# Embedding, state-space layer and routed feed-forward on one core: a rewritten beginning, nine weight copies on ScalarE, the last tile added by TensorE

## The reference

```
h   = W.T[x] + b + positions                    # gather from 50257 x 128
u   = layernorm(h)
Bu  = u @ B_bar.T ; xs = scan(Lambda_bar * x + Bu)   # diagonal complex, 64 states
h   = h + gelu(2 * real(xs @ C.T) + D * u)
xn  = layernorm(h)
top-2 of 8 experts by xn @ router_w.T + router_b, weights = softmax of the two
y_e = (silu(xn @ fc1a_e.T + b1a) * (xn @ fc1b_e.T + b1b)) @ fc2_e.T + b2_e
out = h + sum over the two chosen experts of weight * y_e
```

## Time and profile before

| | us |
|---|---|
| median of 3 runs | 186.21 (184.81 to 190.72) |
| profiled execution: first to last instruction (its span) | 157.3 |
| PE busy in it | 122.2 |
| DVE busy | 114.8 |
| POOL busy | 93.0 |
| ACT busy | 73.4 |
| matmul clock, mean share of full | 0.879 |

### The profile page before, as it was taken

How to read it: one execution, slowest core, us unless ns; L and a number is a source line. 1 busy time by engine, 2 the same in 40 slices (tenths; PEclk the granted TensorE clock), 3 DMA queues, 4 the chain that set the end, 5 groups by cost and what they waited for, 6 DMA issues and landing times.

```text
span 157.3 us, 3532 instructions
## 1 busy us (share of the span) xinstructions
PE 122.2 (78%) x807; PEld 96.5 (61%) x807; DVE 114.8 (73%) x480; ACT 73.4 (47%) x236; POOL 93.0 (59%) x114
## 2 busy tenths in 40 slices
PE   0067896938989968876996899999999999999300
PEld 0022355516837736743894689999999999983000
DVE  0899965899598999878647767587777778734573
ACT  3040882028167106038444356777877777760000
POOL 4778779300077677527756777777777776674000
PEclk9999699997559998589599999999999999997555
DMA  4411111991027271125315412444333111110896
GB/s 118 112 50 36 50 50 46 201 276 52 0 44 230 67 231 60 52 68 108 80 38 133 104 53 69 129 114 116 102 84 94 40 37 50 48 36 0 269 331 201
DMA packets 15093, 15.65 MB, mean 99 GB/s; under 512 B 2995, under 2 KB 11701, under 8 KB 15074
## 3 DMA queue, kind: packets, MB, share of 16 engines
q1 hardware_dynamic: 11058, 9.43, 23.6%
q0 software_dynamic: 2784, 5.28, 10.6%
q10 hardware_dynamic: 1232, 0.72, 1.5%
HBM read 9.62 MB, written 6.27 MB: 101 GB/s over the span
## 4 chain that ended last, share of the span: by engine, by line
PE 23%; issue 9%; DVE 6%; POOL 6%; DMA 5%; DVEq 1%; SPq 1%; ACT 1%; POOLq 0%; ACTq 0%
PE bank L1195 7%; PE bank L1181 7%; PE bank L1171 6%; POOL results L367 6%; DMA yres<-results 3%; DVE act_h L727 1%; PE bank L1161 1%; DMA results<-ysb,dest 1%; SPq L280 1%; DVEq L713 1%; DVE res L820 1%; PE bank L1051 1%; DVE res L824 1%; ACT rows L872 0%; DVE arg L609 0%
## 5 line engine op out<-in xcount | busy, mean ns | idle before, releaser
L356 POOL DMA_INDIRECT sorted_rows<-rows,slot x32 | 32.2, 1007 | 29.1 <-DVE slot L629 20.0
L716 DVE COPY w1b<-w_sb 128x516 f32 x39 | 18.9, 486 | 13.5 <-DVE act_h L727 5.7
L727 DVE SCALAR_TENSOR_TENSOR act_h<-bank,w1b,sil 128x128 f32<-128x128 f32 x78 | 23.6, 343 | 4.8 <-PE bank L1181 1.6
L367 POOL DMA_INDIRECT results<-ysb,dest x22 | 21.6, 983 | 7.9 <-issue 7.3
L1195 PE MATMUL bank<-w_sb,act_h 128*128 x156 | 25.1, 285 | 1.0 <-issue 0.5
L1181 PE MATMUL bank<-xT,w1b 128*128 128x128 f32 x156 | 24.6, 281 | 1.5 <-DVE act_h L727 1.4
L928 ACT ACTIVATE sil<-bank,w1b 128x128 f32<-128x128 f32 x78 | 24.4, 364 | 0.3 <-PE bank L1171 0.2
L1171 PE MATMUL bank<-xT,w1b 128*128 128x128 f32 x156 | 24.4, 280 | 0.0
L1181 PEld LDWEIGHTS bank<-xT,w1b 128*128 128x128 f32 x156 | 21.0, 195 | 2.1 <-DVE act_h L727 2.1
L1195 PEld LDWEIGHTS bank<-w_sb,act_h 128*128 128x128 f32 x156 | 20.9, 195 | 2.0 <-issue 1.9
L367 POOL DMA_INDIRECT results<-ysb,xt x17 | 16.8, 990 | 7.2 <-issue 3.7
(11 more groups left out here) (236 smaller groups left out, 189.7 us busy)
## 6 DMA issues: line engine op xcount, KB each, us to landing
w_sb<-w_all SPq DMA_DIRECT2D x8, 386.0 KB, 5.8
xt<-sorted_rows SPq DMA_DIRECT2D x39, 65.0 KB, 2.0
yres<-results SPq DMA_DIRECT2D x8, 256.0 KB, 4.9
sorted_rows<-pad SPq DMA_DIRECT2D x1, 520.0 KB, 6.6
sorted_rows<-rows,slot POOLq DMA_INDIRECT x32, 2.7
out<-res SPq DMA_DIRECT2D x2, 256.0 KB, 3.9
results<-ysb,dest POOLq DMA_INDIRECT x22
results<-ysb,xt POOLq DMA_INDIRECT x17
```

Of the source, the lines that this page charges most:

```text
L356: gp.indirect_dma_start(sorted_rows[:, :], bass.IndirectOffsetOnAxis(ap=slot[:, k, t:t + 1], axis=0), rows[:, k, t, :], None).then_inc(s_s ...
L367: gp.indirect_dma_start(results[:, :], bass.IndirectOffsetOnAxis(ap=target, axis=0), ysb[i][:, :], None, bounds_check=bound, oob_is_err=Fa ...
L716: v.tensor_copy(w1b[i % 4][:, :], w_sb[:, bass.ds(at, W1)]).then_inc(s_wb, 1)
L727: v.scalar_tensor_tensor(act_h[i % 2][:, q], ps_l[sides(i)][:, q], w1b[i % 4][:, 2 * HID + 2 + c:2 * HID + 3 + c], sil[i % 2][:, q], ALU.a ...
```

## The change

- **Beginning.** `prm` is loaded on ScalarE's queue, ahead of its other loads. VectorE's arithmetic is reordered: the inverse of Lambda and the radius are interleaved with the serial chain of the angle, ahead of group 0's sums; `decay` follows on ScalarE ahead of the group work. `embed_and_inputs` holds only what needs sine and cosine.
- **Gathers.** GpSimd issues all sixteen in a row, its constants after them. It adds positions for group 3 alone; group 2 is added by VectorE.
- **Groups.** `NORMS` pairs x0 with u2 and x1 with u3. On ScalarE and TensorE `normed_u(3)` and `turn_u(3)` come later, the latter between the two halves of `rotated(2)`.
- **Copies.** The weights of tiles 0 to 8 are copied by ScalarE, which reads nine addresses at once. VectorE copies from tile 9 on.
- **Order among first tiles.** On TensorE `turn_last_x` comes behind `first(1)`, and two idle products go. On ScalarE `keep(0)` moves ahead. On GpSimd `scatter_result(1)` comes after `scatter_rows(3)` instead of before.
- **Last tile.** Tile 38 is not scattered. VectorE makes four 128x512 matrices of zeros and ones from its destinations, and TensorE multiplies `ysb` of tile 38 by them into the banks that hold the mixed bias, four banks now instead of two. `results` is zeroed once by a transfer of 2 MB in rows of 2 KB, from a buffer of zeros, since rows of that tile stay unwritten. `add_bias(g)` now stands right ahead of group g's other two additions.

```diff
-NORMS = ["u0", "u1", "x0", "u2", "u3", "x1", "x2", "x3"]
+NORMS = ["u0", "u1", "x0", "u2", "x1", "u3", "x2", "x3"]
+SPREAD = 1
+STORED = NTILES - SPREAD
...
-        ps_add = [banks[0], banks[6]]
+        ps_add = [banks[0], banks[6], banks[2], banks[5]]
...
+        def copied(i):
+            return (s_wa, i + 1) if i < FULL[0] else (s_wb, i - FULL[0] + 1)
...
-            sp.dma_start(prm[:, :], prm_in).then_inc(s_prm, 16)
...
+            sp.wait_ge(s_zero, 1)
+            sp.wait_ge(s_gath[1], 16 * GT)
+            sp.dma_start(results[:, :].rearrange("(p q j) d -> p q (j d)", p=P, j=GT),
+                         zeros[:, None, :].to_broadcast([P, K * NT // GT, GT * D])).then_inc(s_empty, 16)
...
-            sp.wait_ge(s_ys, 16 * NTILES)
+            sp.wait_ge(s_ys, 16 * STORED)
...
-            gather(0)
-            gather(1)
+            for g in range(NG):
+                gather(g)
...
-            gather(2)
-            gather(3)
...
-            for g in (2, 3):
-                pool.wait_ge(s_gath[g], 16 * GT)
-                e = res[:, GT * g:GT * g + GT, :]
-                gp.tensor_tensor(e, e, pos_sb[:, :, :], ALU.add).then_inc(s_emb, 1)
+            pool.wait_ge(s_gath[NG - 1], 16 * GT)
+            e = res[:, GT * (NG - 1):NT, :]
+            gp.tensor_tensor(e, e, pos_sb[:, :, :], ALU.add).then_inc(s_emb, 1)
+            gp.iota(iota_j[:, :, :], [[1, GT], [GT, P]], base=0, channel_multiplier=0,
+                    allow_small_or_imprecise_dtypes=True).then_inc(s_iotaj, 1)
...
+            pool.wait_ge(s_empty, 16)
             scatter_result(0)
-            scatter_result(1)
             scatter_rows(NG - 1)
-            for i in range(2, NTILES):
+            for i in range(1, STORED):
                 scatter_result(i)
...
+            def spread_tile(n, g):
+                dve.wait_ge(s_last, 1)
+                v.tensor_scalar(spread[:, n, g, :], iota_j[:, :, :].rearrange("p j t -> p (j t)"),
+                                last_g[:, n, g:g + 1], None, ALU.is_equal).then_inc(s_spread, 1)
...
             positions_bias()
-            dve.wait_ge(s_rooth, 1)
-            embed_and_radius()
+            embed_and_inputs()
             embed(1)
             norm("u1")
             scan(0)
-            embedded_sums(2)
-            embedded_sums(3)
+            embed(2, GT)
             add_gelu(0)
-            norm("x0", "u2", "u3")
+            norm("x0", "u2")
             scan(1)
             choose(0)
+            embedded_sums(3, GT)
             find_slots(0)
             add_gelu(1)
-            norm("x1")
+            norm("x1", "u3")
...
-            dve.wait_ge(s_table, 2)
-            dve.wait_ge(s_w, 16 * NE)
-            expert_weights(0)
-            expert_weights(1)
             find_slots(2)
...
             for i in range(NTILES):
-                if i + 2 < NTILES:
+                if FULL[0] <= i + 2 < NTILES:
...
+                if i == CHUNKS[-2]:
+                    last_tokens()
+                if i == NTILES - 2:
+                    for t in range(SPREAD):
+                        spread_tile(t, 0)
+
+            for g in range(1, NG):
+                for t in range(SPREAD):
+                    spread_tile(t, g)
             for g in range(NG):
                 add_bias(g)
-            for g in range(NG):
                 dve.wait_ge(s_added, g + 1)
                 dve.wait_ge(s_yl[g][0], 16)
...
+            def copy_weights(i):
+                if i >= 4:
+                    act.wait_ge(s_a, 2 * i - 6)
+                a.copy(w1b[i % 4][:, :], w_sb[:, bass.ds(starts[i], W1)]).then_inc(s_wa, 1)
...
             normed_x(2); copy_xnT(2); second_rows(2)
+            starts = first_list()
+            copy_weights(0)
             gelu(3)
+            copy_weights(1)
+            copy_weights(2)
...
+                if i == 1:
+                    keep(0)
+                if 1 <= i and i + 3 < FULL[0]:
+                    copy_weights(i + 3)
                 if i + 2 < NTILES:
                     turn_copy(i + 2)
                 if i == 0:
+                    copy_weights(3)
                     normed_x(3)
                     copy_xnT(3)
...
-            turn_u(3)
             logits(1)
             rotated(2, 0)
+            turn_u(3)
             rotated(2, 1)
...
+            def spread_result(n, g):
+                pe.wait_ge(s_oe, STORED + n + 1)
+                pe.wait_ge(s_spread, SPREAD * g + n + 1)
+                for j in range(GT):
+                    ins = te.matmul(ps_add[g][:, j * D:(j + 1) * D], spread[:, n, g, j * P:(j + 1) * P],
+                                    ysb[STORED + n][:, :], start=False, stop=(n == SPREAD - 1 and j == GT - 1))
...
-                if i == 0:
-                    idle_products(2, ps_vs)
-                if i == 0:
-                    turn_last_x()
                 if i + 1 < NTILES:
                     first(i + 1)
                 if i == 0:
+                    turn_last_x()
                     list_tiles(1)
```

270 lines of the change are left out of this document (164 added, 106 removed).

## The result

| | us |
|---|---|
| the kernel before, median of 4 runs | 187.98 (184.81 to 190.72) |
| the changed kernel, median of 4 runs | 192.06 (190.86 to 197.73) |
| ratio, 95% interval | 1.0345 (1.025 to 1.044) |
| predicted | 177.0 (174.5 to 181.5) |

Two later comparisons gave 1.0152 (0.995 to 1.035) and 1.0269 (1.016 to 1.038).

What follows compares the result with a forecast made beforehand. GpSimd's own scatter pace was taken to end the run: starts 5.7 us earlier at rows 2, 9.2 at rows 3, 10.5 at the last scatter, less 1.3 in the tail, so 186.2 - 9.2 = 177.0 us, range 174.5 to 181.5.

Steps and rivals of the forecast that it cites:

- The failed step: Beginning, with all gathers in a row taken to lose nothing: `scan(0)` starts at 18.5 for 20.72, gain 2.2 us.
- The sum's base: Whole run: span 157.3 less 9.2, with the same 28.9 us around it, so 186.2 - 9.2 = 177.0 us.
- Group 2's positions, +2.45: VectorE between `scan(0)` and `add_gelu(0)`: 4.1 us become 1.65 with one addition and four sums, gain 2.45 us.
- Eight for twelve, slots(0), `scan(2)`, `turn_u(3)`: Before rows 2: norm of eight tiles +0.35, group 0's slots +0.85, `scan(2)` product wait +0.4, `turn_u(3)` delaying `rotated(2,1)` -0.6 us.
- Rival 1: TensorE's clock stays at half in groups 1 and 2: gain less by 1.3 + 0.4, 178.7 us; chance 0.19.
- Two copies, +0.4: Before slots(2): two weight copies leave VectorE, gain 0.4 us, or 2.0 at full clock.
- Rows 3 at 75.5, "3 us more": GpSimd starts group 3's rows at 75.5 for 84.69, gain 9.2; group 3's slots come 3 us earlier than 78.5.
- 44 x 1.288: Tile loop: GpSimd scatters at its own pace, 56.7 us from rows 3 to the last scatter's start, +1.35 us.
- Tail, -1.3: After the reload: VectorE's four more additions among the loads, two of which count, lose 1.3 us.
- Rival 6: Slower: TensorE's clock falls in the tile loop and stays, 2.90 us a tile for 1.45, 191.5 us; chance 0.04.
- Rival 3: Tail at half clock, or gathers held by the zero fill: 1.5 to 2 us less gain, 178.8 us; chance 0.08.
- rival 5: Fewer VectorE copies make GpSimd's scatters faster, up to 3.9 us, capped by TensorE at some 1.5: 175.5 us; chance 0.02.

Runs made afterwards that it cites:

- e10: Changed kernel with gathers 9 to 16 held until VectorE finished `norm(u1)`: 186.92 us beside 192.0 for the kernel before, ratio 0.9768.
- e9: Changed kernel, unchanged, run again: 193.08 us beside 192.0 for the kernel before, ratio 1.0152.
- e5: Changed kernel with gathers split as before (eight, the constants, the other eight): 187.39 us beside 191.54 for the kernel before, ratio 0.9773.
- e14: e10 with the order of before among the first tiles: 184.04 us beside 186.64 for the kernel before, no interval.
- e17: e14's kernel, unchanged, run again: 184.52 us beside 188.31 for the kernel before, ratio 0.9863.
- e15: e10 with result scatters 1 and on held until the tile list is complete: 186.5 us beside 186.64 for the kernel before, ratio 1.0056.
- e1: Kernel before, unchanged, with a new profile: 188.15 us beside 187.62, ratio 1.0206; span 183.8.
- e7: Kernel before with the weights of tiles 0 to 8 copied by ScalarE: 191.49 us, ratio 1.0006.
- e13: Kernel before with gathers 9 to 16 held until VectorE finished `norm(u1)`: 190.33 us beside 186.64 for the kernel before, ratio 1.0198.
- e4: Kernel before plus the 2 MB zero fill alone, with its memset and the first result scatter's wait: 188.81 us, ratio 1.0268.
- e6: Kernel before with all sixteen gathers in a row, the constants after them: 193.14 us, ratio 1.011.
- e18: Changed kernel, unchanged, run beside e17: 191.3 us beside 188.31 for the kernel before, ratio 1.0269.
- e3: Changed kernel with the weights of tiles 0 to 8 copied by VectorE as before: 193.69 us, ratio 1.0532 to the kernel before.
- e8: Changed kernel with the order of before among the first tiles: 191.18 us beside 191.54 for the kernel before, no interval.
- e12: Changed kernel with the 38 result scatters replaced by SyncE's plain stores to rows in order: one run, 175.76 us.
- e2: Changed kernel with the last tile scattered like the others, no zero fill, no spreading: 191.17 us, ratio 1.0365 to the kernel before.
- e16: e14 with group 3's row paused after four scatters until the tile list is complete: 185.18 us beside 188.31 for the kernel before, ratio 0.9984.
- e11: Changed kernel with groups 2 and 3 loaded by plain transfers from the table's first rows, not gathered by token: one run, 185.59 us.

## Why the prediction was wrong

**The failed step.** The prediction laid the second eight gathers right behind the first ("Gather 12 issues at 12.27 + 4 x 1.26 = 17.3") and costed that at nothing but for the zero fill, with group 1's norm at "3.74" and "VectorE is free at 18.5". The norm took 12.8 us, because the row went on beside it. With the row held back the same list gives 3.45 us and 18.56 (e10). The size at this place is shown by the profiles: five with held gathers have `scan(0)` at 18.6 to 19.7, seven with the row at 27.8 to 28.2.

That step is the difference in sign. In one job the changed kernel takes 193.08 us and the held one 186.92, with 192.0 for the kernel before (e9, e10); with the gathers only split, as they were before, it is 187.39 for 191.54 (e5). Over all jobs the six sets of runs with split or held gathers (e5, e10, e14 to e17) have medians of 184.0 to 187.4, and the changed kernel has 191.3 to 193.1. How much they gain on the kernel before is less sure: 2.3% in two comparisons (e5, e10), nothing in a third (e15), and 1.4% with an interval that takes in 1 in a fourth (e17).

It is not the whole miss. The forecast gain was 9.2 us, and the best of these comparisons gives some 5 by the medians (e10). The rest is in the items below, and in the tile loop.

**The sum's base.** "Span 157.3 ... with the same 28.9 around it" was wrong as well: in the profiled executions of these two kernels 1.7 to 2.4 us lie outside the span, and the spans of e1 and the first profile differ by 26.5 us, which are stops inside the ordinary execution. The prediction used this gap and did not ask what it was. That a profile 29 us shorter than every timed run may be another kind of execution was the warning. In the tile loop, where no row before showed a stop, 10.9 of the 26.5 us go (28 tiles at 1.81 us in e1, 1.42 in the first profile). A gain in place shrinks there and at rows 3, as e10's moments show; what a microsecond at each place is worth in the end was not measured.

**Group 2's positions, +2.45.** In e1 VectorE goes from `scan(0)` to `add_gelu(0)` in 1.6 us without a wait, since GpSimd had time to be done; in the changed kernel in 2.4, with 0.81 for gelu. So -0.8 in these two; e9 has 2.8 us, and e7, with the order of before, 3.2. With held gathers (e10, e13) the addition on VectorE does save 3.6 us of waiting.

**Eight for twelve, slots(0), `scan(2)`, `turn_u(3)`.** Each is worth under 1 us. Rival 1's clock isn't shown to be part of it: the mean granted clock at 30 to 60 us was 1.00, 0.92, 0.86 and 0.85 with the order of before (e1, e4, e6, e7) and 0.85, 0.78 and 0.84 in the changed kernel (changed, e9, e18), at full speed 2.4 GHz. From `scan(0)` to `scan(2)` the profiles overlap (22.5 and 24.6 in e1 and e4, 23.7, 24.2 and 23.9 changed). They stay unsettled.

**Two copies, +0.4.** From `scan(3)` to slots(2) 8.6 to 8.8 us where VectorE copies (e3, e4, e6, e13; e1 10.3), 7.6 to 8.5 where ScalarE does, 7.6 in the changed kernel: 0.1 to 1.2, and the forecast lies in it.

**Rows 3 at 75.5, "3 us more".** Failed. Slots(3) came 18.5 us after slots(2), for 15.05 before and 12 forecast. The copies gained 0.7 to 1.0 in the old order (e7) and 0.3 in the new (e3), the new order of the first tiles took 2.1 (e8, e14). The rest is in e1 too: 17.3 us, with a stop of 4.20 us on VectorE in it.

**"44 x 1.288".** Failed, by the prediction's own sign ("if GpSimd's gaps are longer than 0.3"). The tiles set the pace, at 1.83 us each (e9), and TensorE is busy for 6.27 of 8.00 us, so what bounds the loop is its chain of hand-overs; without GpSimd's scatters beside it, TensorE is busy all the time and a tile takes 1.44 (e12). The 1.45 us a tile of the prediction was a little high, too: the 74 products of the earlier trace rows at 13 a tile are 5.7 tiles and not 5.5, and from `ysb` 10 to 38 the first profile has 1.42.

**Tail, -1.3.** The sign is right, the size low: from the first `yres` sum to the end there are 9.27 us in e1, and 1.3 more in e18, 2.2 in the first profile of the changed kernel and 2.6 in e9. In e2, without the spreading, it is 0.8. In the two longer ones VectorE waits for loads in between, 0.41 and 1.07 us in the first.

**The rivals.** None was this. Rival 6 named the right sign and the wrong place: the clock in the loop is 1.00, and its 191.5 us for a measured 192.06 is luck. Rival 3's zero fill isn't it (e2, e4). On rival 5: the page "SBUF — State Buffer" of the Trainium skill (section "SBUF: two separate sides") says that within the engine side only the port shared by VectorE and GpSimd makes engines wait, and that "PE, ACT, and DVE's dedicated pair never wait on anyone". That lock doesn't show in the scatters, whose median is 0.97 or 0.98 us with and without a weight copy beside them (first profile, e1, e14). And it doesn't explain the stops: VectorE stands for 8.29 us and ScalarE for 10.21 (e14) while GpSimd goes on. The page speaks of ports, and no run shows that these stops are waits for one, so they don't contradict it.

**What stays open.** Which part of the chip holds the waits. The releaser reads "remote", so no engine of the program. The queues that the profile calls "instruction" moved the same 7 and 12 packets in the same 0.3 and 0.2% of the time in the first profile and in e1, so slower loading of instructions doesn't show there; that it starts later isn't excluded. And why the first profile of the kernel before had the same rows of gathers and scatters and no stop: something beside the row must be needed for the stops, and no run here varied it. The time of that execution isn't on record either.

## What to carry to other kernels

In this kernel a row of indirect transfers from GpSimd was not free for the others. Ask of such a row what stands beside it, a chain of small dependent steps above all, and price the edit by a profile that has both. Holding a row back can cost as much at another place (e13). Before working from a profile, hold its span against the timed runs; a gap of 15% is a finding, not an offset. A stop that depends on a row moves when the row is moved (e16), so count where it lands. And run the kernel before against itself: here it differed by 2% (e1), and `scan(0)` by 3.7 us (e1, e7).

## What the runs showed of the hardware

All of this holds for the ordinary executions; the first profile of the kernel before has the same rows and none of it.

- While GpSimd issues indirect transfers back to back (0.95 to 0.97 + 0.30 us each), hand-overs even from one VectorE instruction to the next, which show no wait in the first profile, take 1.0 to 1.3 us (e6). Later in a row VectorE and ScalarE stand for 3 to 10 us (changed, e14), and TensorE with them.
- The longest of these stops end 0.6 to 2.0 us after the row: it ends at 99.57 and work goes on at 100.55 (e14), 98.98 and 100.53 (e15), 93.29 and 94.52 (e16), 22.99 and 24.95 (changed), 24.20 and 26.12 (e7), 23.31 and 23.90 (e6). Shorter ones end within a row, as at 20.75 in the changed kernel.
- The same bytes by plain transfers of SyncE leave little of it: one wait of 0.81 us in e11, and 1.44 us a tile for 1.83 in e12.
- A row of eight beside operations on 128x512 cost VectorE little: in e10 it went from 18.51 to 29.3, beside `scan(0)` to `add_gelu(0)`, and the next stretched operation was one of 1.21 us at 31.21. In e17 ScalarE had a stop of 1.74 us in the same place, to 29.33.
